# The second sequence's input, statistics, turns and query/key products ahead of the first attention

## The reference

```
for L in 0..3:
    sh, sc, g, sh2, sc2, g2 = split(silu(c) @ w_ada + b_ada, 6)
    h = layernorm(x) * (1 + sc) + sh
    q, k, v = split(h @ w_qkv + b_qkv)                     # 16 heads of 18
    o = softmax(q k^T / sqrt(18)) v                        # layers 0, 1, 3: over the 512 tokens
    x = x + g * (o @ w_o + b_o)                            # layer 2: between the 16 heads of each token
    h = layernorm(x) * (1 + sc2) + sh2
    x = x + g2 * ffn(h)                                    # 288 -> 1152 -> 288, gelu
```

## Time and profile before

| | us |
|---|---|
| median of 3 runs | 2240.1 (2237.44 to 2245.22) |
| the profiled execution's own time | 2242.45 |
| its span | 2240.7 |
| PE busy | 2031.2 (91%) |
| DVE busy | 1334.0 (60%) |
| ACT busy | 1142.2 (51%) |
| POOL busy | 207.1 (9%) |

### The profile page before, as it was taken

How to read it: one execution, slowest core, us unless ns; L and a number is a source line. 1 busy time by engine, 2 the same in 40 slices (tenths; PEclk the granted TensorE clock), 3 DMA queues, 4 the chain that set the end, 5 groups by cost and what they waited for, 6 DMA issues and landing times.

```text
span 2240.7 us, 38982 instructions
## 1 busy us (share of the span) xinstructions
PE 2031.2 (91%) x15592; PEld 1502.5 (67%) x15592; DVE 1334.0 (60%) x2940; ACT 1142.2 (51%) x1705; POOL 207.1 (9%) x311
## 2 busy tenths in 40 slices
PE   6988999989998999999899899899888898899998
PEld 4346478658965995798474647788786556464658
DVE  4747647756674767576665763453454848584832
ACT  2353734564655456545627374552543554746363
POOL 3000011112100211011020000002000000000001
PEclk8586999999989999999989999998999898999899
DMA  5234232352324233333423223436345141313101
GB/s 161 58 115 84 81 115 71 60 143 76 90 51 133 72 89 65 109 103 78 115 54 59 79 24 59 92 56 123 50 80 131 8 124 25 107 16 108 16 3 25
DMA packets 204731, 173.97 MB, mean 78 GB/s; under 512 B 54822, under 2 KB 164678, under 8 KB 204550
## 3 DMA queue, kind: packets, MB, share of 16 engines
q1 hardware_dynamic: 197974, 158.76, 30.2%
q0 software_dynamic: 6576, 12.71, 2.0%
HBM read 125.57 MB, written 40.11 MB: 74 GB/s over the span
## 4 chain that ended last, share of the span: by engine, by line
PE 64%; DVE 17%; ACT 11%; DMA 3%; issue 2%; SPq 2%; POOL 0%; ACTq 0%; POOLq 0%; DVEq 0%
PE PSA L1857 16%; PE PSA L1872 14%; DVE MX L1497 7%; PE PSA L1761 6%; PE PSA L1648 5%; PE PSA L1738 5%; PE PSA L1751 4%; ACT PB L1346 4%; PE PSA L1708 4%; PE PSA L1720 2%; PE PSA L1781 1%; PE PSA L1671 1%; DVE HH L1627 1%; ACT FH L1376 1%; DVE FL L1397 1%
## 5 line engine op out<-in xcount | busy, mean ns | idle before, releaser
L1497 DVE TENSOR_REDUCE MX<-PSA 128x1 f32<-128x512 f32 x768 | 490.1, 682 | 294.0 <-PE PSA L1738 290.3
L1857 PE MATMUL PSA<-A,FH 128*128 128x256 f32 x2520 | 442.6, 291 | 14.3 <-DVE HH L1627 11.4
L1872 PE MATMUL PSA<-FH,HH 128*128 128x288 f32 x2016 | 448.2, 313 | 2.0 <-DVE HH L1627 2.0
L1383 ACT ACTIVATE HH<-PSA 128x512 fp32r<-128x512 f32 x252 | 150.5, 597 | 568.9 <-PE PSA L1857 560.4
L1346 ACT ACTIVATE PB<-PSA 128x1024 f32<-128x1024 f32 x384 | 370.8, 1024 | 122.4 <-PE PSA L1751 121.7
L1857 PEld LDWEIGHTS PSA<-A,FH 128*128 128x128 f32 x2520 | 363.0, 194 | 36.7 <-issue 18.5
L1872 PEld LDWEIGHTS PSA<-FH,HH 128*128 128x128 f32 x2016 | 329.6, 195 | 43.0 <-issue 38.6
L1872 PE MATMUL PSA<-FL,HH 128*128 128x288 f32 x1008 | 303.8, 301 | 0.0
L1738 PE MATMUL PSA<-KS,QS 54*128 54x512 f32 x768 | 224.4, 518 | 34.2 <-DVE MX L1497 11.5
L1256 POOL TENSOR_TENSOR X<-X,TM 128x288 f32<-128x288 f32 x128 | 100.6, 804 | 1476.7 <-DVE TM L1562 1476.7
L1761 PE MATMUL PSA<-PB,VT 128*32 128x512 f32 x1536 | 225.6, 653 | 0.0
(11 more groups left out here) (166 smaller groups left out, 2246.4 us busy)
## 6 DMA issues: line engine op xcount, KB each, us to landing
qkd<-HH SPq DMA_DIRECT2D x48, 504.0 KB
ST<-in_L_cond_w SPq DMA_DIRECT2D x51, 432.0 KB
ST<-in_L_cond_w SPq DMA_DIRECT2D x102, 192.0 KB
QS<-qkd SPq DMA_DIRECT2D x88, 144.0 KB
KS<-qkd SPq DMA_DIRECT2D x88, 144.0 KB
QS<-qkd SPq DMA_DIRECT2D x144, 72.0 KB
KS<-qkd SPq DMA_DIRECT2D x144, 72.0 KB
ST<-in_L_cond_w SPq DMA_DIRECT2D x153, 48.0 KB
```

Of the source, the lines that this page charges most:

```text
L1383: e.activation(r(HH[u][:, 0, :]), PS[bk][:, :], gelu)
L1497: e.reduce_max(MX[p // 2 % 2][:, col:col + 1], PS[bk][:, :], axis=AX.X).then_inc(free[bk], 1)
L1857: m = e.matmul(PS[bk][:, s_ * 256:(s_ + 1) * 256], r(w_), r(x_[:, half * 256:(half + 1) * 256]), start=(z == 0), stop=(z == 6))
L1872: m = e.matmul(PS[bk][:, 0:C], r(HH[u][:, c, tk]), r(w_), start=False, stop=(j == NCH - 1 and z == 2))
```

## The change

The setup before the first attention gets sequence 1's share. Its input is loaded right behind the first two weight jobs; its statistics stand between the turn and the query/key products of sequence 0; its normalised rows, turns and five query/key products come before V of sequence 0. The loads of its groups of QS and KS stay behind attention 0's use of these groups and so are no longer among the products (`at_end`). The second part of ada (mean and scale vectors, job 2) moves ahead of V's weights (job 3), and both are issued by SP.

```
--- before.py
+++ after.py
@@ -33,7 +33,7 @@
 QK_LAND = 12000
 STK_LAND = 16000
 ST_LAND = 14000
-SP_JOBS = 3
+SP_JOBS = 4
 BG = 3
 TURN_AT = 2
 LEAD = 6
@@ -130,7 +130,7 @@
         ring_n[0] += 1
         return bank(ring_of[0][ring_n[0] % len(ring_of[0])])
 
-    jobs = [("ada", 0, 0), ("q", 0), ("v", 0), ("ada", 0, 1), ("ada", 0, 2), ("wg",), ("p", 0)]
+    jobs = [("ada", 0, 0), ("q", 0), ("ada", 0, 1), ("v", 0), ("ada", 0, 2), ("wg",), ("p", 0)]
     jobs += [("f", k) for k in range(3)]
     k_ = 3
     for i_ in range(NI + 1):
@@ -325,7 +325,7 @@
         qk_at[i, grp] = pe[0]
         put("qkin", i, p0, p1, grp, outs, s2_done[3 if i == 12 else p1 // 2 - 1])
 
-    at_end = (0,)
+    at_end = (0, 1)
 
     def proj_qk2(i):
         for t in range(5):
@@ -370,12 +370,13 @@
                 qk_in(i, 2, 4, 1, outs[3])
         if i == 12:
             return
-        if i:
-            while s2_at[0] < (i - 1, 3):
-                yield
-        else:
-            qk_in(i, 0, 2, 0, outs[1])
-            qk_in(i, 2, 4, 1, outs[3])
+        for g in range(2):
+            if i in at_end:
+                while i and s2_at[0] < (i - 1, g):
+                    yield
+                qk_in(i, 2 * g, 2 * g + 2, g, outs[2 * g + 1])
+        while i and s2_at[0] < (i - 1, 3):
+            yield
         qk_in(i, 4, 8, 2, outs[4])
         qkd_free[i % 2] = tuple(qk_n)
         yield
@@ -759,6 +760,7 @@
     put("x", 0)
     ahead()
     ahead()
+    put("x", 1)
     drain(stats(0, 1))
     ada0 = ada(0)
     for _ in range(3):
@@ -766,12 +768,16 @@
     drain(split(("q", 0), "q"))
     normed(0, 1, n_norm[0])
     drain(turn_x(norm_of[0], 0, 0, 0, 0))
+    drain(stats(1, 0))
     drain(proj_qk(0))
-    drain(split(("v", 0), "v"))
-    proj_v(0)
-    put("x", 1)
+    normed(1, 0, n_norm[0])
     for _ in range(3):
         next(ada0)
+    drain(split(("v", 0), "v"))
+    pre1 = pre(1)
+    for _ in range(3 + 5 + 1):
+        next(pre1)
+    proj_v(0)
     put("msk")
     forced[0] = False
     bg += [ada0, split(("wg",), "wg"), split(("p", 0), "p")]
@@ -782,7 +788,7 @@
         if i < NI:
             nxt = pre(i + 1) if i + 1 < NI else iter(())
             if i == 0:
-                nxt = itertools.chain(norm(1), nxt)
+                nxt = pre1
             if i + 1 < NI and (i + 1) // 4 != 2:
                 stream.append(s1_steps(i + 1))
             ring_of[0] = RING_A2 if L == 2 else RING_A
```

## The result

The changed kernel is slower. The four first executions have a median of 2261.7 us (2257.9 to 2265.0) against 2242.2; the ratio is 1.0072, some 16 us, with a 95% interval of 1.0039 to 1.0105. One of the twelve, at 2281.6 us, counts as a slow execution and is left out of this ratio. Weighted by the inverse squares of the half intervals the two make 1.0052 ± 0.0019, or +11.6 ± 4 us. The forecast was +12.0, 2252.

A forecast was written before the change was run, and what follows sets the result against it. Bounds by stretch: the wait for KS, DVE's row maxima, PE at 1.2 GHz, ACT, then DVE. Terms 25.9 + 0.8 − 9.6 + 1.0 − 3.0 − 3.1 = +12.0 on 2240.1 give 2252; own range 2247 to 2259, outer 2238 to 2264.

The forecast's parts named there:

- Up to 34.1: Sequence 0's query/key products: DVE does sequence 1's statistics first, the delay is made up; cost 0 (bounds 0 and 1).
- Start of the first score: From the products' end to the first score: PE's added work and late stores move it from 48.0 to 73.9, +25.9 us.
- the hold: Before V of sequence 0: its bank waits for copies held by stores behind 36 loads; 15.2 us beyond PE's own 10.7.
- Rival (a): Output DMAs land early, 5.2 us after issue: start moves by 17.7, sum +3.8, 2244; chance 0.20.
- (b): Outputs are no bound: only PE's own 10.7 are added at the start, sum −3.2, 2237; chance 0.07.
- Attention 0: Stall of 2.15 goes (−2.2), eleven pairs of sequence 1 scores in steps 10 to 15 cost +3.0; together +0.8 (−4 to +9).
- rival (d): The clock rises earlier, so five steps of 5.0 us at 1.2 GHz take about 3.2: some −10, 2242; chance 0.10.
- Rival (c): The clock falls in attention 0's second half, six steps of 5.0 instead of 3.7: +8, 2260; chance 0.11.
- V of sequence 1: Sign at the end of attention 0: it comes right behind the last output turn, at about 163.
- End of attention 0: The 11.0 us of turns and products before V go, some 1.4 come in sight: −9.6 (−8 to −11).
- Middle: Sequence 1's first-pass scores after attention 0, bound by DVE: 19 steps instead of 17, three better placed; +1.0 (−2 to +4).
- First expert and attention 1: Fewer first-pass score steps there: first expert 2 instead of 8, −3.0; attention 1 3 remain, −3.1 (0 to −6).

The follow-up runs named there:

- five_hh: Changed kernel with the fourth and fifth query/key product of sequence 1 in two extra buffers, so no copy waits for a store; ratio 0.9989 to the kernel before.
- stores_first: Changed kernel with 24 of the 36 loads issued behind the stores of sequence 1's products on SP's queue; ratio 1.0029 to the kernel before.
- v_first: Changed kernel with V of sequence 0 ahead of the turns and query/key products of sequence 1; ratio 1.0034 to the kernel before.
- v_mid_again: Second run of v_mid_five, no edit; ratio 0.9997 to the kernel before.
- jobs_only: Kernel before with only ada 1 ahead of V's weights and products, both loaded by SP, nothing of sequence 1 moved; ratio 1.0010.
- again: The changed kernel run once more, no edit; ratio 1.0042 to the kernel before.
- v_mid_five: five_hh with V of sequence 0 between the turns and the query/key products of sequence 1; ratio 0.9974 to the kernel before.

## Why the prediction was right

*Up to 34.1 (0 to 1).* The last product ends at 34.9 instead of 34.1. DVE's statistics came first as foreseen; one small wait was not in my text, the copy of the fifth product for the store of the second (2.2 us, at 36.18). It delayed the loads' first issue from 36.74 to 38.33.

*Start of the first score (+25.9).* Measured +26.4 and +24.0. Step by step: copies at 64.8 and 67.1 foreseen, 65.33 and 66.71 measured; V from 68.4 to 73.9 foreseen, 68.16 to 74.4 measured. The products ended at 55.3, not 52.5, since they began at 44.7 and ran partly at 1.2 GHz, but this lay under the hold. five_hh shows the two parts apart: +13.4 without the hold, where I had 10.7, and 10.6 to 13.0 for the hold, where I had 15.2. Both were missed, in opposite directions. The second output followed the first by 1.4 us, less than my 2.3. The estimate of 1.8 by the Trainium skill, page "DMA: Bandwidth & Descriptors" (Why a DMA increments its semaphore by 16 and not by 1), was nearer. The page's number of shares is borne out, since the semaphore has fourteen updates after the first. The text does not say by what rate 36.9 KB make 1.8 us; by the earlier trace rows, 221 GB/s over 16 engines that are busy for 0.71, it is 1.9. What the same page says on order (Queues, rings and completion order) agrees with the rows of 12.4 us behind the loads and at most 3.7 ahead of most of them. Rival (a), landing in 5.2, fails in the changed kernel. Its condition, no loads ahead, is what stores_first made, nearly: the start there is +12.7 where (a) had +17.7, as no copy waits any more. In (b) I gave only PE's 10.7 to the start and 2237 to the sum; five_hh is that case, with +13.4 at the start and a ratio of 0.9989, which is 2238 on the median of 2240.1.

*Attention 0 (+0.8).* This term is off: it measured −4.1 and −7.4, and the miss is in its first half. From the first second-pass score to the ninth product the changed kernel gained 9.3 and 9.7 us (26.3 to 17.0, 23.8 to 14.1), where I had 2.2. The rest is rival (d): the clock stood at 0.50 until 99 us before, until 108 and 104 in the two executions after, so that a program that is 24 to 26 us behind has fewer steps of 5.0 us left. I had priced it at 10 and given it 0.10. Two other runs bear this out. PE's instructions stand in one order in stores_first and five_hh, and their first second-pass scores start within 0.8 us of each other (79.3 and 80.0). In stores_first the clock rose at 110, its first five attention-by-value products came 5.0, 5.0, 5.0 and 3.8 us apart, and it gained 3.1 up to the ninth. In five_hh the clock rose at 95, the same products came 4.7, 3.1, 3.2 and 2.1 apart, and it gained 9.1. That PE's long busy stretch of the earlier trace rows kept a clock of 0.50 told me nothing on when it rises. The second half cost +5.2 and +2.3; I had 3.0. Rival (c), a fall of the clock there, priced at 8, did not come in these two profiles, but it did in three others: in v_first, five_hh and v_mid_again the clock was at 0.50 for 14 to 17 us in this half, which cost +9.3, +10.0 and +10.0. V of sequence 1 came at 157.5 and 152.0, not at 163, by what the first half gained.

*End of attention 0 (−9.6).* −10.4 and −10.1 (from the sixteenth product to V).

*Middle (+1.0).* +2.5 and +3.3: the stretch of the earlier trace rows is 43.6 us for 40.7. DVE is not as full there as I had supposed: 31.7 us of 43.6, where it was 32.1 of 40.7. What holds the rest stays open.

*First expert and attention 1 (−3.0 and −3.1).* Together −7.9 and −8.5 from 198.6 to 299.1.

By these rows the sum at 299 us is +6.4 in one profile and +1.1 in the other, less than 12.0, since the clock gave 7 back in attention 0. The timed executions say +11.6 ± 4. Two things may make up the distance, and neither is shown. The profile of before may be late at that place (jobs_only −3.5). And it may be a lucky one behind it: twelve of the thirteen other profiles lose ground to it from 467 us on, where PE's steps are the same (jobs_only 3.2, again 2.9, the first profile 12.8), and its clock of 0.91 between 1500 and 1750 us is above the 0.87 and 0.90 of the two after. A second profile of the kernel before would tell how much of this is the draw; it was not taken. So the forecast of the time and of its cause was right, and the term of the start to 2 us. The closeness of the sum is partly luck, inside the start by two errors of opposite sign, and in the whole because attention 0 was mis-sized by 5 to 8, in the direction of a gain. The first four executions alone have a median of 2261.7, above the forecast's own range (2247 to 2259) and inside the outer one (2238 to 2264); only with the twelve more does the cost lie beside +12.

## What to carry to other kernels

Before work is moved ahead, walk every queue that it passes, and above all the one that frees its buffers: a store behind 36 loads freed its buffer 12.4 us after its issue instead of 3.7 and held PE, DVE and ACT at once, and either two idle buffers or 24 loads moved behind it brought the first score forward by 11 to 14 us, with no change to the work. A product that took PE 1.6 us ahead of the attention took it 3.0 to 5.3 with its wait among the scores (1.9 + 1.1, 3.3 + 2.0), by the clock and by the ring of banks. What such a wait costs depends on what bounds the stage: among the first-pass scores, where DVE is the bound, a product delayed their end by 1.7 us in the first case and by 4.0 in the second. Where a kernel's executions differ by 1%, compare the same place in several profiles before a late difference is explained.

## What the runs showed of the hardware

The time at 1.2 GHz differed between two executions of one and the same program by 38 us (321.3 and 283.4) and in v_mid_five by 49 (261.4 and 310.1), and the spans by 17.7 and 20.9. The long stretch at 0.50 in the first scores and attention 0 ended at 87 to 113 us. In the five profiles whose first score starts at 48 to 50 it ended at 95 on average (90 to 103), in the three at 72 to 75 at 108 (104 to 113): between these groups, which are of different programs, the start moved by 25 us and the rise by 13. The start alone doesn't set it: with first scores at 60.7 and 61.4 and PE's instructions in one order, stores_first had the rise at 110 and five_hh at 95. A store of 504 KB freed its buffer in 3.7 us or less where the twelve loads ahead of it had been issued 6 us and more before, while 36 loads right ahead of it made it 12.4; nine of its fourteen shares came with the end of the loads, and five landed within 3.1 us of its issue.
